# SyncE passes the release of gather buffers on to GpSimd

## The reference, cut to what matters

```
xn  = layernorm(x)
agg = segment_sum(xn[dst], src, 6250)               # rows gathered by dst, summed by src
x   = x + ((agg + xn) @ gW1 + gb1) @ gW2 + gb2
y   = layernorm(x)
w   = softmax(mean(y[None], 0) @ Wr + br)            # 8 experts
h   = relu(bn1(y @ W1[e] + b1[e]))                   # 256 -> 256
h   = relu(bn2(h @ W2[e] + b2[e]))                   # 256 -> 256
out = x + sum over e of w[:, e] * (h @ Wo[e] + bo[e])
```

## Time and profile before

| | us |
|---|---|
| median of 3 runs (lowest, highest) | 1777.59 (1771.95, 1782.02) |
| the profiled execution, its own time | 1778.76 |
| its span, first to last instruction | 1776.9 |

### The profile page before, as it was taken

The page is one execution under the profiler, slowest core; times in us unless marked ns, Lnnn a source line. Parts: engine busy times, 40 slices in busy tenths (PEclk is TensorE's granted clock), DMA queues, the critical chain, the costliest instruction groups (busy, mean ns, idle before and its releaser), DMA issues.

```text
span 1776.9 us, 27488 instructions
## 1 busy us (share of the span) xinstructions
PE 1256.6 (71%) x7858; PEld 791.1 (45%) x7858; DVE 1262.7 (71%) x3045; ACT 875.0 (49%) x1593; POOL 982.9 (55%) x1001
## 2 busy tenths in 40 slices
PE   0144444433578888787887878878788788889996
PEld 0134334211345545454554545545445454555665
DVE  7999999443476767766777767777667777676555
ACT  7948551000145545454454544455445555456777
POOL 2042992766576666666666656666566666660000
PEclk9967555655699999999999999999999999999999
DMA  7020341433332333333333323333233333342000
GB/s 212 0 71 31 136 142 30 115 89 92 86 89 84 100 96 85 112 86 89 108 85 113 87 85 107 87 111 87 82 111 87 112 88 99 99 81 42 1 16 16
DMA packets 84065, 153.17 MB, mean 86 GB/s; under 512 B 18151, under 2 KB 56330, under 8 KB 83908
## 3 DMA queue, kind: packets, MB, share of 16 engines
q0 software_dynamic: 40608, 110.94, 22.8%
q1 hardware_dynamic: 43300, 40.36, 7.3%
HBM read 131.97 MB, written 19.27 MB: 85 GB/s over the span
## 4 chain that ended last, share of the span: by engine, by line
PE 42%; DVE 26%; issue 12%; another core or an unknown queue 11%; ACT 5%; DVEq 2%; DMA 1%; ACTq 0%; SPq 0%
PE PL L1335 9%; PE PB L1318 8%; DVE acc L917 7%; PE PA L1303 7%; PE PN L1235 6%; PE PN L1234 5%; DVE zz L665 5%; DVE zz L666 5%; PE PT L1259 3%; ACT junk L486 2%; DVE xt L1023 2%; DVE onehot L847 1%; ACT zz L559 1%; DVEq L900 1%
## 5 line engine op out<-in xcount | busy, mean ns | idle before, releaser
L424 POOL DMA_INDIRECT gbuf<-xn_hilo,dsti x846 | 842.1, 995 | 483.9 <-issue 198.3
L917 DVE TENSOR_TENSOR acc<-acc,PN 128x256 f32 x798 | 332.8, 417 | 292.4 <-remote 134.8
L1234 PE MATMUL PN<-gbuf,onehot 128*128 128x256 f16 x798 | 211.6, 287 | 267.0 <-DVE acc L917 184.9
L558 ACT ACTIVATE h<-PA,bnt,bns 128x512 f16<-128x512 f32 (+1 forms) x208 | 156.5, 752 | 350.7 <-PE PA L1303 234.5
L1335 PE MATMUL PL<-wsplit,h 128*128 128x256 f16 x2352 | 296.4, 277 | 11.3 <-DVE h L1008 4.2
L1303 PE MATMUL PA<-yT,wsplit 128*128 128x512 f16 (+1 forms) x1248 | 292.4, 373 | 11.6 <-issue 11.6
L1318 PE MATMUL PB<-h,wsplit 128*128 128x512 f16 (+1 forms) x1248 | 285.9, 368 | 0.0
L572 ACT ACTIVATE h<-PB,bnt,bns 128x512 f16<-128x512 f32 (+1 forms) x208 | 156.2, 751 | 237.9 <-PE PB L1318 229.3
L1234 PEld LDWEIGHTS PN<-gbuf,onehot 128*128 128x128 f16 x798 | 79.5, 100 | 426.6 <-DVE acc L917 248.6
L1335 PEld LDWEIGHTS PL<-wsplit,h 128*128 128x128 f16 x2352 | 231.4, 99 | 50.8 <-ACT zz L573 10.5
L1235 PE MATMUL PN<-gbuf,onehot 128*128 128x256 f16 x798 | 210.5, 286 | 0.0
(11 more groups left out here) (214 smaller groups left out, 1236.9 us busy)
## 6 DMA issues: line engine op xcount, KB each, us to landing
gbuf<-xn_hilo,dsti POOLq DMA_INDIRECT x846
x_plus_bias<-xst SPq DMA_DIRECT2D x49, 128.0 KB, 1.7
xn_hilo<-onehot SPq DMA_DIRECT2D x49, 128.0 KB, 1.7
xt<-x_plus_bias SPq DMA_DIRECT2D x49, 128.0 KB
out<-xt SPq DMA_DIRECT2D x49, 128.0 KB
acc<-in_x SPq DMA_DIRECT2D x4, 1536.0 KB
h<-in_L_ffn_W SPq DMA_DIRECT2D x16, 256.0 KB, 2.8
h<-in_L_ffn_Wo SPq DMA_DIRECT2D x8, 256.0 KB, 2.7
```

The source lines that it names most:

```text
L424: pool.indirect_dma_start(gbuf[:, k % SLOTS, :], None, xn_dram, bass.IndirectOffsetOnAxis(dsti[:, k:k + 1], 0)).then_inc(gat[k % SLOTS], 16)
L917: V.tensor_tensor(to, to, bank[:, i, :], ALU.add).then_inc(s["acc_done"], 1)
L1234: T_.matmul(bank[:, m % 2, :], onehot[:, par, m, :], gbuf[:, k, 0:D], start=True, stop=False)
```

## The change

POOL no longer waits for `ent_done`. SP does: for each pair of each chunk it waits until the pair's last entry is through, then raises a new semaphore `slot_free` by one, and POOL waits for that, counted in pairs. The releases of 20 chunks stand behind SP's first two `load_x`. From group 1 on SP runs `group(g, ...)`: releases of the first two chunks, store of group g - 1, releases of the third chunk, the wait for that store, load of group g + 1, and the releases of the five other chunks. So each store stands behind the first two chunks of the next group, where it was first in line, and each load behind its third. The order of SP's last loads and stores, from store 10 on, is unchanged.

```diff
-            "oh_ready", "select", "own", "nmr_ready", "max_ready", "bo_split", "ent_done", "acc_done",
+            "oh_ready", "select", "own", "nmr_ready", "max_ready", "bo_split", "ent_done", "slot_free", "acc_done",
...
+            def release(c, n):
+
+                for i in range(n):
+                    for p in PAIRS:
+                        sp.wait_ge(s["ent_done"], c * EPC + (i * EPC + p[-1] + 1))
+                        sp.sem_inc(s["slot_free"], 1)
+
+            def group(g, par, rounds):
+
+                release(PRO + EX * g, 2)
+                store(g - 1, GT, 1 - par)
+                release(PRO + EX * g + 2, 1)
+                sp.wait_ge(s[f"out{1 - par}"], rounds * (16 * GT))
+                load_x(g + 1, GT, 1 - par)
+                release(PRO + EX * g + 3, EX - 3)
+
             load_x(0, GT, 0)
             load_x(1, GT, 1)
-            store(0, GT, 0)
-            sp.wait_ge(s["out0"], 16 * GT)
-            load_x(2, GT, 0)
-            store(1, GT, 1)
+            release(0, PRO + EX)
+            group(1, 1, 1)
             with sp.Fori(1, GROUPS // 2 - 1) as q:
-                sp.wait_ge(s["out1"], q * (16 * GT))
-                load_x(2 * q + 1, GT, 1)
-                store(2 * q, GT, 0)
-                sp.wait_ge(s["out0"], q * (16 * GT) + 16 * GT)
-                load_x(2 * q + 2, GT, 0)
-                store(2 * q + 1, GT, 1)
+                group(2 * q, 0, q)
+                group(2 * q + 1, 1, q + 1)
+            store(GROUPS - 3, GT, 1)
             sp.wait_ge(s["out1"], 16 * GT * (GROUPS // 2 - 1))
...
-                for p in PAIRS:
+                for i, p in enumerate(PAIRS):
                     if k >= SLOTS and m == p[0]:
-                        pool.wait_ge(s["ent_done"], k - SLOTS + len(p))
+                        pool.wait_ge(s["slot_free"], (c - 2) * len(PAIRS) + i + 1)
```

## The result

The changed kernel takes **1799.02 us** (median, 1794.63 to 1807.76), the kernel before beside it 1778.46 us (1771.95 to 1782.02): a ratio of 1.0132 with a 95% interval of 1.0109 to 1.0154 (the two medians by themselves give 1.0116). That is about 21 us slower, where 11 us were forecast. The profiled execution of after took 1807.76 us (span 1805.9, again 1.9 around it), at the top of its runs and 29.0 us over the profiled one of before; differences between the two traces are thus larger than those of the medians. New are SP's wait and increment in L315 and L316.

A forecast was written before the change was run, and what follows sets the result against it. It took the loop of PE and DVE as the bound, PE's reports being held up while POOL gathers back to back. Hop 9 us plus first stage 2 us made 11 on 1777.6: forecast 1788 us, range 1745 to 1820.

The forecast's parts named there:

- store and load, moved: SP's stores and loads now stand before releases; each may hold one by 2.6 to 3 us, hidden, costed at nothing.
- POOL's spare 2.8 us a chunk: A chunk takes 14.1 us, its nine gathers 11.3; POOL can use the rest to make up for being late.
- the 28 us: How early a gather is issued before its use, the time 18 entries take; taken to hide a late gather.
- uncovered case: Ten stores, ten loads at 2.5 us and four SP loop branches at 3.6 us, if nothing hid them: 64 us.
- The hop: Each release goes PE, SP, POOL: 0.2 us later; a quarter of the long stage's pauses on the path, 9 us.
- 182 pauses: POOL's waits in the long stage with gathers, 222.2 us in all; forecast to remain, each starting 0.2 us later.
- The first stage: First twelve chunks, 312 to 490 us: 11 of 17 POOL pauses start 0.2 us later, 2 us.
- SP's own instructions: On SP: only releases, stores and loads wait behind its waits; four loop branches of 3.6 us taken as hidden.
- A: Whole kernel: nothing moves because gathers are issued 28 us ahead, 1778 us; chance 0.12.
- B: SP's 460 waits and increments join the held-up queue; a tenth of 322 us, 32 us, gives 1811 us; chance 0.10.
- C: PE and DVE's pair loop: later POOL starts let more reports out, saving 24 us, 1753 us; chance 0.18.
- D: POOL's own waiting for PE's semaphore delays PE's reports; first stage saves 43, DVE's waits 97: 1639 us; chance 0.10.

The follow-up runs named there:

- e7: Kernel before, SP untouched; POOL writes scratch tiles ahead of the first gather waiting for a group's third and fourth chunk, so it starts late: 1806.4 us.
- e1: Changed kernel, but POOL waits for `ent_done` itself at the pairs of a group's third and fourth chunk; other releases pass through SP: 1785.6 us.
- e2: Changed kernel, but POOL waits for `ent_done` itself everywhere; SP keeps its waits, increments and new places of stores and loads: 1779.8 us.
- e3: Changed kernel, but only releases of a group's third and fourth chunk pass through SP; POOL reads `ent_done` itself at all others: 1800.5 us.
- e6: Kernel before, but POOL waits for DVE's addition of the pair (`acc_done`) instead of PE's entry matmuls: 1879.6 us.
- e9: Kernel before with a 128x256 scratch write on POOL behind every gather from the second group on: 1758.3 us.
- e12: Changed kernel with a 128x256 scratch write on POOL behind every gather from the second group on: 1778.9 us.
- e14: Changed kernel, POOL waiting for `ent_done` itself, with a 128x256 write behind every gather from the groups on: 1794.9 us (kernel before 1792.1).
- e15: Changed kernel, only a group's third and fourth chunk released through SP, with a 128x256 write behind every gather: 1796.2 us (kernel before 1792.1).
- e5: Kernel before with gathers 19 to 846 left out, entry matmuls reusing the first 18 tiles (sums not the reference's): 1528.6 us.
- e16: Same kernel as e9, run again in the last comparison: 1698.0 us, ratio 1.0748 to the kernel before at 1580.8 us.
- e11: Kernel before with a 128x256 write only behind gathers that wait for a group's third, fourth and fifth chunk: 1776.1 us.
- e8: Changed kernel with a 128x256 write behind gathers that wait for a group's third, fourth and fifth chunk: 1788.5 us.

## Why the prediction was wrong

The sign was right, with a chance of only 0.38 (same had 0.34), and the measured 1799.0 us lies in the range, but the size is about twice the 11 us.

- **The step that failed** is *store and load, moved*: each "can hold a release by at most its own length, 2.6 to 3 us, once; POOL's spare 2.8 us a chunk and the 28 us hide this". Its size was right: the gathers behind the store and the load come 1.6 and 1.2 us later than before. That it is hidden was wrong. The 28 us do cover the data (no list of PE's waits in after names a gather), and yet the time was lost. e7 shows this without SP: 2.6 us of lateness a group (1.61 ahead of e = 2, 0.97 ahead of e = 3: 756.93 against 755.96) cost 3.3 us a group, nothing of it hidden. The term was costed at nothing; it is 13 to 21 us by e1, e2 and e3. Why is argued and not shown: the spare 2.8 us a chunk are the pauses in which PE's reports get through, and making up for a late start spends them. The prediction had said this of the hop (its pauses) and not applied it here. The 64 us given for the uncovered case were three times too high or more.
- *The hop* was taken at 0.2 us. After a pause POOL starts 0.172 us behind DVE's start in after and 0.138 in before (medians): 34 ns, below the lower end of 0.1. A quarter of the 182 pauses at this would be 1.5 us and all of them 6.2. The hops outside e = 2 and 3 cost 5.8 us by medians (e1 less e2), which would put nearly every pause on the path and not a quarter. But two things speak against reading it so: a group is no longer in e1's trace than in e2's (111.00 and 111.39 us), and e6's price, 103 us for 1.22 us at each pause, gives 2.9 us for 34 ns. So the hop was taken six times too long, what share of the pauses counts is open, and that 9 us were forecast and 5.8 measured is partly luck.
- *The first stage* was given 2 us and shows -0.3.
- *SP's own instructions* were costed at nothing but for the hop; e2 has 3.7 us (interval 0.9 to 6.7), not separated into waits and new places.
- *A* (nothing moves) fell with e7: the lead does not hide lateness. *B* (SP's instructions in the held-up queue): its 460 increments take 17 ns each, and all of SP's part without the hop costs 3.7 us (e2), not 32. *C*: DVE's waits with no releaser found rose from 97.0 to 116.7 us, where under 75 was its sign; but e9 shows that a gain by spacing is there to be had. *D*: POOL no longer reads PE's semaphore in after and the late reports are all there. Its 1639 us, meant as what would be left without late reports, is 58 us above the 1580.8 of the comparison in which they are missing.
- Of the signs named, 182 pauses (186), SP's releases of tens of ns and DVE's waits up by 10 us (11.1) came; POOL at 0.34 us behind DVE did not. Neither a wait of PE for a gather nor a late load at `linear_add` came, the two signs of "wrong altogether": the cover failed although both were absent.

**Open.** Why the change costs 20 us where gathers are spaced (e12 against e9), with 26 reports over 2 us late against 16, and whether that is SP's part, the held releases or the hop. The chunks of e12's trace and the 1.3 us between e14 and e15 speak against the held releases; e14 and e15 lack e9 beside them, and in the last comparison no release was waited for. Why e2's late gathers at e = 2 cost so little. And what makes the reports late at all; only that gathers must be running (e5) and that it isn't enough (e16) is shown. The count of reports over 2 us late orders most kernels as their times do, but not all: e11 has 20 at 1776.1 us and e8 23 at 1788.5.

## What to carry to other kernels

A deep buffer and an engine's spare time are no proof that a late start is hidden: delay the start by itself, as e7 does, before you count on it, and ask what happens in the pauses that catching up will spend. When a release is passed on by a third engine, the hop itself (34 ns here) can matter less than what that engine does between two releases (four DMAs, 2 to 2.4 us, here): release between the DMAs, or keep the direct wait. And a gain that comes from dodging such an effect (the writes: 1.0% faster in one comparison, 7.5% slower where the effect is missing) has to be tried on more than one chip and at more than one time before it is kept; between the relay and the direct wait of the kernel before, the direct wait is the one to keep.

## What the runs showed of the hardware

- With gathers running, TensorE's semaphore updates reached VectorE, ScalarE and GpSimd late, together, whatever the semaphore: at 751.42 to 751.74 us in e7 for a pair that ended at 748.99. Over 320 pairs of the kernel before, the time from the end of a pair's last matmul to DVE's addition has a median of 0.5 us and goes up to 3.4; without gathers (e5) the median is 0.14. In another comparison a kernel that had such delays in e9 (16 of 320 over 2 us) had none of them in e16. The kernel before took 1777.5 us in the one and 1580.8 in the other; that all of these 197 us are the late reports is not shown.
- GpSimd waiting for VectorE's addition and not for TensorE's matmul, 1.22 us later for a pair of two, costs 103 us, although each gather is issued two chunks ahead of its use.
- A relay through SyncE (wait, increment, wait) added 34 ns to a release in the median; its increments took 17 ns in all 460 cases.
- A write of 128x256 f32 on GpSimd between two gathers takes 0.33 us and moves their starts from 1.25 to 1.44 us apart. After six gathers without a pause, a report came 2.6 us late.
